# A mixture-of-experts layer on one core: the experts' first layer with tokens as stationary operand and a transpose of its result, in place of staged weights

## The reference, cut to what matters

```
def _L0_ffn_ref(x, conf_w, conf_b, gate_w, up_w, down_w, wealth):
    bids = sigmoid(x @ conf_w.T + conf_b) * wealth          # [tokens, 8]
    top_bids, selected = top_k(bids, 2)
    combine = sum(one_hot(selected, 8) * softmax(top_bids)[..., None])
    def ffn(gw, uw, dw):                                    # gw, uw [512, 128], dw [128, 512]
        return (silu(x @ gw.T) * (x @ uw.T)) @ dw.T
    return sum over experts of combine * ffn(...)
```

## Time and profile before

| | us |
|---|---|
| median of 3 runs | 520.24 (517.69 to 520.26) |
| the profiled execution, its own time | 522.8 |
| its span, first to last instruction | 521.0 |
| first matmul of gate(0), last matmul group of gate(38) start at | 365.14, 498.08 |
| last scatter issued at | 503.25 |

### The profile page before, as it was taken

The page is one execution under the profiler, slowest core; times in us unless marked ns, Lnnn a source line. Parts: engine busy times, 40 slices in busy tenths (PEclk is TensorE's granted clock), DMA queues, the critical chain, the costliest instruction groups (busy, mean ns, idle before and its releaser), DMA issues. The chain is left out here.

```text
span 521.0 us, 11219 instructions
## 1 busy us (share of the span) xinstructions
PE 466.1 (89%) x4008; PEld 328.7 (63%) x4008; DVE 347.9 (67%) x631; ACT 314.4 (60%) x636; POOL 184.3 (35%) x328
## 2 busy tenths in 40 slices
PE   7999999999999999999999999679887777877850
PEld 7755555555555555565555555669787777877850
DVE  7897898888888897997898862775233332332325
ACT  2257787777777777877777876202455444454513
POOL 8142402332332422512501220143455555555520
PEclk9999999999999999999999999686999999999985
DMA  7503134243342342322122100431111111111117
GB/s 194 144 24 99 42 103 116 63 121 98 83 126 72 99 123 80 98 67 72 44 66 54 40 3 1 149 94 10 42 38 34 39 37 41 37 34 37 35 30 238
DMA packets 27305, 38.13 MB, mean 73 GB/s; under 512 B 5540, under 2 KB 14500, under 8 KB 27252
## 3 DMA queue, kind: packets, MB, share of 16 engines
q1 hardware_dynamic: 21780, 29.74, 21.2%
q0 software_dynamic: 2496, 5.12, 3.7%
q10 hardware_dynamic: 2976, 2.56, 1.6%
HBM read 16.52 MB, written 4.65 MB: 41 GB/s over the span
## 5 line engine op out<-in xcount | busy, mean ns | idle before, releaser
L517 DVE TENSOR_REDUCE max_part<-max_ps 128x2 f32<-128x1024 f32 (+1 forms) x192 | 225.5, 1218 | 33.2 <-PE max_ps L676 27.7
L475 ACT ACTIVATE probs<-ring_ps 128x512 f32<-128x512 f32 x374 | 194.1, 603 | 49.6 <-PE ring_ps L699 45.2
L699 PE MATMUL ring_ps<-blocks,keys 64*128 64x512 f32 x374 | 145.1, 465 | 0.0
L709 PE MATMUL pv_ps<-probs,value_cols 128*32 128x256 f32 x1536 | 102.9, 385 | 0.3 <-ACT probs L475 0.3
L676 PE MATMUL max_ps<-keys,blocks 64*128 64x512 f32 x256 | 81.3, 425 | 0.6 <-DVE max_part L517 0.6
L699 PEld LDWEIGHTS ring_ps<-blocks,keys 64*128 64x128 f32 x374 | 63.1, 183 | 26.2 <-ACT probs L475 20.8
L1162 DVE COPY xT<-t_ps 128x128 f32<-128x128 f32 x39 | 11.4, 291 | 94.7 <-remote 55.4
L709 PEld LDWEIGHTS pv_ps<-probs,value_cols 128*32 128x32 f32 x1536 | 40.0, 109 | 40.8 <-ACT probs L475 13.1
L1249 PE MATMUL gate_ps<-xT,staged 128*128 128x128 f32 x312 | 43.1, 281 | 23.4 <-DVE xT L1162 23.0
L376 POOL CAST maxes<-rowmax 128x8 fp32r<-128x8 f32 x32 | 6.3, 197 | 150.8 <-DVE rowmax L524 150.8
L1010 POOL DMA_INDIRECT pick_outs<-y_out,target x39 | 38.4, 985 | 55.0 <-DVE y_out L1178 47.6
(11 more groups left out here) (179 smaller groups left out, 529.0 us busy)
## 6 DMA issues: line engine op xcount, KB each, us to landing
keys<-parts SPq DMA_DIRECT2D x96, 96.0 KB
blocks<-masked SPq DMA_DIRECT2D x93, 64.0 KB
ctx_v_sb<-ctx_v_dram SPq DMA_DIRECT2D x8, 256.0 KB, 2.9
gate<-gateT_dram SPq DMA_DIRECT2D x8, 256.0 KB, 2.9
up<-upT_dram SPq DMA_DIRECT2D x8, 256.0 KB, 2.9
raw<-ctx_kT_dram SPq DMA_DIRECT2D x7, 256.0 KB, 2.8
y_in<-pick_outs SPq DMA_DIRECT2D x4, 256.0 KB, 6.4
y_in<-pick_outs ACTq DMA_DIRECT2D x4, 256.0 KB, 6.8
```

Of the source, the lines that this page charges most:

```text
L475: act.activation(probs[par][:, k, PAIR * a:PAIR * (a + 1)], bank("exp", s * XUNITS + u)[:].rearrange("p (g n) -> p g n", n=N), ACT.Exp).th ...
L517: vec.reduce_max(out, bank, axis=AX.X).then_inc(max_done, 1)
L699: pe.matmul(ps[:], keys[rows, t, k * P:(k + 1) * P], blocks[rows, t], start=True, stop=True)\
L709: mm = pe.matmul(pv_ps[ROWS * g:ROWS * (g + 1), 0:N], value_cols[:, t, k, g, :], probs[q % 2][:, k, g, :], start=(k == 0), stop=(k == KT - 1))
```

## The change

Tokens become the stationary operand of the first layer, and the expert's weights move past them straight out of `m.gate` and `m.up`, picked by a register: one 512-column product for gate and one for up. The result then has the tokens on the partitions, so the activated hidden units are transposed by PE in four 128-column transposes into a new pair of PSUM banks `at_ps`, and ACT copies them into `hiddenT`. The staging copies on ACT are gone. The second layer runs two slots behind the first instead of one, the pipeline is drained over two steps instead of one, DVE multiplies ahead of its copy of the next tokens, and the idle matmuls write to `at_ps[0]`.

```diff
--- before.py
+++ after.py
@@ -887,7 +887,7 @@
         xT_filled, xT_copied = sem("xT_filled"), sem("xT_copied")
         gate_filled, up_filled = sem("gate_filled"), sem("up_filled")
         silu_done, act_done = sem("silu_done"), sem("act_done")
-        gate_staged, up_staged = sem("gate_staged"), sem("up_staged")
+        actT_filled, actT_copied = sem("actT_filled"), sem("actT_copied")
         y_filled, y_copied = sem("y_filled"), sem("y_copied")
         second_weighted = sem("second_weighted")
         first_added, summed, stored = sem("first_added"), sem("summed"), sem("stored")
@@ -927,13 +927,13 @@
         table = sb("table", [1, SLOTS_PAD], I32)
         x_in = sb("x_in", [P, 4, C])
         xT = sb("xT", [P, 2, P])
-        silu, staged = sb("silu", [P, 2, I]), sb("staged", [P, 2, 2, I])
+        silu, hidden = sb("silu", [P, 2, I]), sb("hidden", [P, 2, I])
         hiddenT = sb("hiddenT", [P, 2, IC, P])
         y_out = sb("y_out", [P, 4, C])
         y_in = sb("y_in", [P, 2, TILES, C])
         t_ps = [psum(f"t_ps{i}") for i in range(2)]
         gate_ps, up_ps = [psum(f"gate_ps{i}") for i in range(2)], [psum(f"up_ps{i}") for i in range(2)]
-        spare_ps = psum("spare_ps")
+        at_ps = [psum(f"at_ps{i}") for i in range(2)]
         xT_ps, y_ps = t_ps
         CONSTS = 8
         block = ctx.enter_context(nc.Block())
@@ -1028,27 +1028,19 @@
             act.wait_ge(gap_ready, 2)
             act.activation(weight[:], gap[:], ACT.Sigmoid).then_inc(weights_done, 1)
 
-            def stage(j, r):
-                e = act.value_load(table[0:1, bass.ds(j, 1)], min_val=0, max_val=E - 1)
-                wait_for(act, up_filled, j - 1)
-                act.activation(staged[:, r % 2, 0], m.gate[:, bass.ds(e, 1), :].rearrange("p a i -> p (a i)"), ACT.Copy)\
-                   .then_inc(gate_staged, 1)
-                act.activation(staged[:, r % 2, 1], m.up[:, bass.ds(e, 1), :].rearrange("p a i -> p (a i)"), ACT.Copy)\
-                   .then_inc(up_staged, 1)
-
             def step(i, r):
                 j = 4 * i + r
-                if exists(i, r, 1):
-                    stage(j + 1, r + 1)
                 if exists(i, r, 0):
                     act.wait_ge(gate_filled, j + 1)
                     wait_for(act, act_done, j - 1)
                     act.activation(silu[:, r % 2, :], gate_ps[r % 2][:], ACT.Silu).then_inc(silu_done, 1)
-
-            act.wait_ge(table_ready, 1)
-            act.wait_ge(m.gate_up_in, 32 * E)
-            stage(0, 0)
-            slots(step, SLOTS)
+                if exists(i, r, -1):
+                    act.wait_ge(actT_filled, j)
+                    wait_for(act, y_filled, j - 2)
+                    act.activation(hiddenT[:, (r - 1) % 2], at_ps[(r - 1) % 2][:].rearrange("p (c n) -> p c n", n=P),
+                                   ACT.Copy).then_inc(actT_copied, 1)
+
+            slots(step, SLOTS + 1)
             def weigh_second(c):
                 act.wait_ge(y_loaded[2 * c + 1], 16)
                 for t in range(c * CHUNK, (c + 1) * CHUNK):
@@ -1163,22 +1155,22 @@
 
             def step(i, r):
                 j = 4 * i + r
-                if exists(i, r, 1):
-                    copy_xT(j + 1, r + 1)
                 if exists(i, r, 0):
                     vec.wait_ge(silu_done, j + 1)
                     vec.wait_ge(up_filled, j + 1)
-                    wait_for(vec, y_filled, j - 1)
-                    vec.tensor_tensor(hiddenT[:, r % 2].rearrange("p c n -> p (c n)"), up_ps[r % 2][:], silu[:, r % 2, :], ALU.mult)\
+                    wait_for(vec, actT_filled, j - 1)
+                    vec.tensor_tensor(hidden[:, r % 2, :], up_ps[r % 2][:], silu[:, r % 2, :], ALU.mult)\
                        .then_inc(act_done, 1)
-                if exists(i, r, -1):
-                    vec.wait_ge(y_filled, j)
-                    if j >= 5:
-                        vec.wait_ge(y_stored[(r - 1) % 4], (i if r >= 1 else i - 1) * 16)
-                    vec.tensor_copy(y_out[:, (r - 1) % 4, :], y_ps[:, 0:C]).then_inc(y_copied, 1)
+                if exists(i, r, 1):
+                    copy_xT(j + 1, r + 1)
+                if exists(i, r, -2):
+                    vec.wait_ge(y_filled, j - 1)
+                    if j >= 6:
+                        vec.wait_ge(y_stored[(r - 2) % 4], (i if r >= 2 else i - 1) * 16)
+                    vec.tensor_copy(y_out[:, (r - 2) % 4, :], y_ps[:, 0:C]).then_inc(y_copied, 1)
 
             copy_xT(0, 0)
-            slots(step, SLOTS + 1)
+            slots(step, SLOTS + 2)
             vec.wait_ge(weights_done, 1)
             for c in range(CHUNKS):
                 vec.wait_ge(y_loaded[2 * c], 16)
@@ -1194,7 +1186,7 @@
         def _(pe):
             def idle(turns):
                 for _ in range(turns):
-                    pe.matmul(spare_ps[:, 0:P], m.ident[:], m.ident[:], start=True, stop=True)
+                    pe.matmul(at_ps[0][:, 0:P], m.ident[:], m.ident[:], start=True, stop=True)
 
             idle(4)
             pe.wait_ge(late_norm, QT)
@@ -1244,35 +1236,38 @@
                 wait_for(pe, xT_copied, j)
                 pe.transpose(xT_ps[:, 0:P], x_in[:, r4, :], m.ident[:]).then_inc(xT_filled, 1)
 
-            def hidden_rows(ps, weights, x):
-                for c in range(IC):
-                    mm = pe.matmul(ps[:, c * P:(c + 1) * P], weights[:, c * P:(c + 1) * P], x, start=True, stop=True)
-                return mm
-
             def step(i, r):
                 j = 4 * i + r
                 if exists(i, r, 0):
+                    e = expert(j)
                     pe.wait_ge(xT_copied, j + 1)
-                    pe.wait_ge(gate_staged, j + 1)
                     wait_for(pe, silu_done, j - 1)
-                    hidden_rows(gate_ps[r % 2], staged[:, r % 2, 0], xT[:, r % 2, :]).then_inc(gate_filled, 1)
-                    pe.wait_ge(up_staged, j + 1)
+                    pe.matmul(gate_ps[r % 2][:], xT[:, r % 2, :], m.gate[:, bass.ds(e, 1), :].rearrange("p a i -> p (a i)"),
+                              start=True, stop=True).then_inc(gate_filled, 1)
                     wait_for(pe, act_done, j - 1)
-                    hidden_rows(up_ps[r % 2], staged[:, r % 2, 1], xT[:, r % 2, :]).then_inc(up_filled, 1)
+                    pe.matmul(up_ps[r % 2][:], xT[:, r % 2, :], m.up[:, bass.ds(e, 1), :].rearrange("p a i -> p (a i)"),
+                              start=True, stop=True).then_inc(up_filled, 1)
                 if exists(i, r, 1):
                     transpose_x(i, r, 1)
-                if exists(i, r, -1):
-                    e = expert(j - 1)
-                    pe.wait_ge(act_done, j)
-                    wait_for(pe, y_copied, j - 1)
+                if exists(i, r, -2):
+                    e = expert(j - 2)
+                    pe.wait_ge(actT_copied, j - 1)
+                    wait_for(pe, y_copied, j - 2)
                     for c in range(IC):
-                        mm = pe.matmul(y_ps[:, 0:C], hiddenT[:, (r - 1) % 2, c, :],
+                        mm = pe.matmul(y_ps[:, 0:C], hiddenT[:, r % 2, c, :],
                                        down[:, bass.ds(e, 1), c, :].rearrange("p a h -> p (a h)"),
                                        start=(c == 0), stop=(c == IC - 1))
                     mm.then_inc(y_filled, 1)
+                if exists(i, r, -1):
+                    pe.wait_ge(act_done, j)
+                    wait_for(pe, actT_copied, j - 2)
+                    for c in range(IC):
+                        mm = pe.transpose(at_ps[(r - 1) % 2][:, c * P:(c + 1) * P],
+                                          hidden[:, (r - 1) % 2, c * P:(c + 1) * P], m.ident[:])
+                    mm.then_inc(actT_filled, 1)
 
             transpose_x(0, 0, 0)
-            slots(step, SLOTS + 1)
+            slots(step, SLOTS + 2)
 
 
 def kernel(x, ctx_2048, L0_xattn_w_qkv, L0_xattn_w_proj, L0_xattn_b_proj, L0_ffn_conf_w, L0_ffn_conf_b,
```

## The result

| | before | changed |
|---|---|---|
| median | 520.11 us (517.69 to 520.26, 4 runs) | 513.12 us (512.59 to 513.85, 4 runs) |
| ratio, with its 95% interval | | 0.9876 [0.9852, 0.9899] |
| span of the profiled execution | 521.0 us | 511.2 us |
| gate(0) and gate(38) start on PE | 365.14, 498.08 | 365.86, 486.20 |
| last scatter | 503.25 | 494.30 |

The account below looks back on a forecast made before the run. PE was not the bound in the mean: its late-announced results lost 0.71 us a slot. Slots at 38 x 3.85 added 13.4 us, the drain 1.75, together 15.1 on the median 520.24: 535 us, range 508 to 543.

Parts of the forecast that it names:

- I take 3.85, the low end: Mean slot time with the hold in about every second slot: 3.85 us, from 3.85 to 4.1; chance 0.45.
- the hold: PE's results announced 1.4 and 1.9 us late in every second slot, read as bound to POOL's gapless indirect DMAs.
- The rival's condition: On POOL, the next scatter 1.88 us after the gather starts must be far enough, against 1.89 that a hold lasts.
- With no pause: On POOL in the held slot, the scatter comes 1.40 us after the gather's start, without idle time before it.
- the alternation sustains itself: Argument against the hold going: after a held slot the next scatter comes early, 2.69 us apart, as before.
- PE in all, 3.17: PE's work in a slot: 1.72 + 0.11 + 0.90 + 0.44 = 3.17 us, 0.38 more than before.
- Covered steps: In clean slots, DVE's new order, the later second layer and ACT's removed staging were to cost or gain zero.
- The drain, 6.92: From the last gate to the last scatter: 6.92 us against 5.17 before, +1.75 us once.
- The hold-free rival, 509.5: No slot is held, each takes 3.17 us: -12.5 us, with the drain -10.7, giving 509.5; chance 0.31.
- The rule on semaphore increments: PE's increments rise from four to five a slot; if the hold grew with them, a slot takes 4.06 us.
- The clock: Rival that PE's clock falls to 1.2 GHz: 6.3 us a slot, run about 628 us; chance 0.02.

## Why the prediction was wrong

- **"I take 3.85, the low end"**: this step failed, with the case under it, that the hold stays in about every second slot. Slots took 120.34 / 38 = 3.17 us. In their place stood slots without a hold: each takes what PE's parts add up to, 38 x (3.85 - 3.17), some 26 us less than forecast. The number was worked out as if held slots were given, while the rival that had them gone stood at a chance of 0.31. Why they are gone stays open; the runs show what does not decide it, and the pattern above. The rival's condition was half read: I compared gather to next scatter, 1.88 against 1.89, and called the margin nil. The kernels with a memset show that this distance alone does not decide (held at 1.68, free at 1.47). "With no pause" ahead of the scatter of 388.82 was misread too: the earlier trace rows have POOL idle for 0.43 us there. And the argument that "the alternation sustains itself" was taken from the old layout, where PE runs ahead of a delayed scatter; in the new one no slot started it.
- **PE in all, 3.17**: right. Gate to up 0.86 (400.92 to 401.78), transposes 0.44 (403.64 to 404.08), the slot 3.16.
- **Covered steps** (product ahead of the token copy, second layer two slots behind, staging gone): right in steady slots; PE is busy for 3.17 of 3.17. Waits for the token copy showed at the start, where gate(1) comes 3.12 behind gate(0) and waits 1.03, and gate(2) waits 0.59. Staging was priced at nothing: moving it ahead gave nothing (523.22 beside 522.8, one run), leaving it out took 2.7 us off the held kernel (517.63 beside 520.34).
- **The drain, 6.92**: mis-sized, 8.10. The second layer of slot 37 waits for ACT's copy of its own transposes, which I had as done, just as that of slot 38 does, where the sum has the wait:

```profile
490.18 1.15 PE L1257 MATMUL t_ps<-down,hiddenT 128*128 x8 [0.77 <-ACT hiddenT L1040]
...
492.54 1.15 PE L1257 MATMUL t_ps<-down,hiddenT 128*128 x8 [0.77 <-ACT hiddenT L1040]
```

  The first of them was left out of the sum (0.8 us: PE begins at 490.18 and not at 489.37); the rest is 0.1 in single steps, such as 1.19 from the last second layer's start to DVE's copy (492.54 to 493.73), where the sum has 1.07.
- **The hold-free rival, 509.5**: the right outcome, 3.6 us low against 513.1. Its difference of -10.7 was nearly that of the two profiled executions, -9.8 (the drain cost 1.2 more, the rest -0.2). But the profiled execution of before stood 2.6 above its median, and that of the changed kernel, 512.96, at its own; so the medians differ by 7.0 only, and adding the difference to the median carried the 2.6 over.
- **The rule on semaphore increments**: PE makes five a slot in place of four and no slot is held. The Trainium skill's page VectorE: DVE Perf Modes, section on the TRN2 errata, warns that one engine's increments at a high rate can deadlock another. The hold scaled by their number gave 4.06 us a slot; the measured 3.17 says that their number does not size this hold.
- **The clock**: granted 1.00 in both slots of the stretch above, at 2.4 GHz, as said.

The forecast also took one thing for granted that no row of one trace can show: that the time of the kernel before is a property of the kernel. In the group without the hold it took 495.4 us, and there the sum of PE's parts is the whole story: 38 x 0.38 = 14.4, with the drain's 2.9 it gives 512.7 for the new layout, and its variant with a memset measured 512.6.

## What to carry to other kernels

When an engine is idle in a stretch because a result is announced late, ask first how far away its reader stands: moving one transpose ahead of the gate product, four lines, took 10 us off the old kernel, where the rewriting of the layer took off 7.0 and 9.6. Work added to such an engine is paid out of its idle time as long as the stall stays (16.7 us of work for 1.7 us); where there is no stall, the 0.38 us a slot that the new layout adds showed in full. And if a kernel has a self-sustaining pattern of stalls, measure it on more than one chip before taking its time as the reference: here the new layout gained 1.2% and 1.8% in two measurements where the old one is held, and its variant with a memset lost 3.4% on the chip where it is not.

## What the hardware did that was not expected

- The kernel before took 520.28, 522.54, 522.8 and 520.34 us in four groups of runs, each on another chip, and 495.37 on a fifth. The changed kernel took 513.12 and 512.94; its variant with the memset took 511.91 on a chip with the hold and 512.58 on the one without, so the new layout hardly notices which chip it is. Each group was one chip in one session, so the two cannot be told apart.
- On chips with the hold results of PE are announced late, in before by 1.4 us (gate) and 1.9 (token transpose); without the gathers none is (2.79 us a slot, one run).
- With the tokens as stationary operand, the same products cut into four of 128 columns cost more than in one piece: slots of 3.33 us against 3.16, and 0.99 from gate to up against 0.86. Why was not tried.
- The version with the early transpose was not run on the chip without the hold; what it takes there is open. Open too is what in the chip delays the announcements.
